# Moving one group's attention stage one to three beats later in a decoder-layer kernel, with the exponential's table loaded ahead of the first softmax

## The reference, cut to what matters

```
# stage 1, linear attention: 16 heads of 8
q, k = sigmoid(n @ Wq + bq), sigmoid(n @ Wk + bk);  v, h = n @ Wv + bv, n @ Wh + bh
attn = (q (k^T v)) / (q sum(k));  gated = layernorm(attn) * (h + beta)
x1   = x + relu(gated @ Wo + bo)
# cross attention to ctx (128 keys of width 96), 16 heads of 64
x2   = x1 + softmax(Q K^T / 8) V @ XWo + Xbo,   Q from layernorm(x1), K and V from ctx
# feed-forward: a shared one and the best of 8 experts
out  = x2 + shared(layernorm(x2)) + expert[argmax](layernorm(x2))
```

## Time and profile before

| | us |
|---|---|
| median of three runs | 604.29 (603.48 to 604.79) |
| the profiled execution | 604.9 |
| its span | 603.2 |
| PE busy, share of the span | 576.2, 96% |
| DVE busy | 432.7, 72% |
| ACT busy | 432.1, 72% |
| POOL busy | 306.9, 51% |
| share of PE in the chain that ended last | 67% |
| mean granted TensorE clock | 0.993 of full |

### The profile page before, as it was taken

The page is one execution under the profiler, slowest core; times in us unless marked ns, Lnnn a source line. Parts: engine busy times, 40 slices in busy tenths (PEclk is TensorE's granted clock), DMA queues, the critical chain, the costliest instruction groups (busy, mean ns, idle before and its releaser), DMA issues.

```text
span 603.2 us, 15181 instructions
## 1 busy us (share of the span) xinstructions
PE 576.2 (96%) x5479; PEld 529.2 (88%) x5479; DVE 432.7 (72%) x1214; ACT 432.1 (72%) x1514; POOL 306.9 (51%) x328
## 2 busy tenths in 40 slices
PE   7978999999999999999999999999999999999993
PEld 7867998998999899988899898988998988899893
DVE  3868666878686768766877777676857459689773
ACT  2668778777876777676867687768776876777771
POOL 3544653365336743475256544563365336246774
PEclk9998999999999999999999999999999999999998
DMA  7530000000000000010000000000040021252530
GB/s 153 136 76 14 18 2 1 15 19 2 1 15 28 28 2 14 19 33 6 14 20 26 11 2 15 19 19 2 24 136 20 7 65 37 68 144 80 151 101 15
DMA packets 24955, 23.52 MB, mean 39 GB/s; under 512 B 7007, under 2 KB 22497, under 8 KB 24880
## 3 DMA queue, kind: packets, MB, share of 16 engines
q1 hardware_dynamic: 21520, 15.96, 10.1%
q0 software_dynamic: 2784, 6.32, 3.0%
q10 hardware_dynamic: 576, 0.26, 0.6%
HBM read 15.03 MB, written 7.95 MB: 38 GB/s over the span
## 4 chain that ended last, share of the span: by engine, by line
PE 67%; ACT 16%; DVE 10%; DMA 3%; issue 2%; POOL 1%; SPq 1%; POOLq 0%; DVEq 0%
PE bank L1451 8%; PE bank L1429 8%; PE bank L1416 8%; PE bank L1440 8%; PE bank L1277 7%; ACT prob L1147 7%; PE bank L1279 6%; PE bank L1278 6%; PE bank L1565 4%; PE bank L1295 2%; PE bank L1397 2%; PE bank L1582 2%; ACT probT L1153 2%; PE bank L1283 2%; ACT L1118 1%
## 5 line engine op out<-in xcount | busy, mean ns | idle before, releaser
L1147 ACT ACTIVATE prob<-bank,mneg 128x128 f32<-128x128 f32 x512 | 183.3, 387 | 65.1 <-DVE mneg L866 64.9
L604 POOL TENSOR_TENSOR prob<-prob,rden 128x512 f32<-128x512 f32 x124 | 126.6, 1041 | 102.7 <-DVE rden L873 102.6
L1147 ACT ACTIVATION_READ_ACCUMULATOR prob<-bank,mneg 128x1 f32 x512 | 115.3, 225 | 0.0
L1153 ACT COPY probT<-bank 128x512 f32<-128x512 f32 x128 | 77.6, 608 | 16.3 <-PE bank L1429 15.6
L866 DVE TENSOR_REDUCE mneg<-bank 128x4 f32<-128x512 f32 x128 | 83.0, 670 | 2.7 <-PE bank L1416 2.5
L1429 PE MATMUL bank<-ident,prob 128*128 128x128 f32 x512 | 78.4, 276 | 1.8 <-ACT probT L1153 0.7
L543 POOL TENSOR_TENSOR rstd<-var_eps,neg_half 128x4 f32<-128x4 f32 x24 | 24.7, 1030 | 99.1 <-DVE var_eps L700 99.1
L1429 PEld LDWEIGHTS bank<-ident,prob 128*128 128x128 f32 x512 | 59.8, 142 | 8.4 <-issue 2.9
L1416 PE MATMUL bank<-kT,qT 64*128 64x128 f32 x1024 | 65.9, 279 | 0.0
L1416 PEld LDWEIGHTS bank<-kT,qT 64*128 64x128 f32 x1024 | 59.8, 188 | 5.8 <-issue 2.5
L1451 PE MATMUL bank<-xwo,oT 128*128 128x128 f32 x512 | 63.7, 277 | 0.4 <-issue 0.4
(11 more groups left out here) (225 smaller groups left out, 1391.3 us busy)
## 6 DMA issues: line engine op xcount, KB each, us to landing
prob<-routed SPq DMA_DIRECT2D x39, 128.5 KB, 2.3
s_work<-in_x_dram SPq DMA_DIRECT2D x8, 256.0 KB, 2.9
ctx_nat<-in_ctx_dram SPq DMA_DIRECT2D x8, 192.0 KB, 2.6
routed<-blank SPq DMA_DIRECT2D x9, 128.5 KB, 3.5
s_work<-in_L_ffn_rt_gate_dram SPq DMA_DIRECT2D x1, 1024.0 KB, 5.5
s_work<-in_L_ffn_rt_up_dram SPq DMA_DIRECT2D x1, 1024.0 KB, 9.5
prob<-in_L_xattn_Wq_dram SPq DMA_DIRECT2D x1, 512.0 KB, 6.8
xwo<-in_L_xattn_Wo_dram SPq DMA_DIRECT2D x1, 512.0 KB, 9.7
```

Of the source, the lines that this page charges most:

```text
L604: nc.gpsimd.tensor_tensor(view, view, spread(rden[:, m % 2, c * NC:(c + 1) * NC], 2, S), ALU.mult)\
L1147: last = nc.scalar.activation(prob[:, m % 2, p * S:(p + 1) * S], score_bank[c][:, i * S:(i + 1) * S], ACT.Exp, bias=mneg[:, m % 2, p:p + 1 ...
L1153: nc.scalar.copy(probT[:, m % 2, c * 512:(c + 1) * 512], made(r1, ("T", m, c))[:])\
```

## The change

It adds entries for group 1 to `MOVED`, changes one, moves the two halves of the feed-forward's weight split, and adds one activation that makes the compiler load the exponential's table there.

```
@@ MOVED
-                 (1, "turn x"): (-2, 3), (1, "copy x^T"): (-2, 3), (1, "x^T low"): (-2, 3),
+                 (1, "turn x"): (-2, 3), (1, "copy x^T"): (-2, 3), (1, "x^T low"): (-1, 0),
...
+                 (1, "sigmoids"): (-1, 3), (1, "k^T v"): (0, 0), (1, "mask"): (0, 0), (1, "q k^T v"): (0, 1),
+                 (1, "attention"): (0, 1), (1, "gate terms"): (0, 0), (1, "rstd of attention"): (0, 1),
+                 (1, "gating, first half"): (0, 2), (1, "gating, second half"): (0, 2),
+                 (1, "turn gated"): (1, 0), (1, "copy gated^T"): (1, 0), (1, "output"): (1, 1), (1, "x1"): (1, 1),
+                 (1, "rstd of x1"): (1, 1), (1, "normalise x1"): (1, 1), (1, "turn x1"): (1, 3),
+                 (1, "x1^T high"): (1, 3), (1, "x1^T low"): (1, 3)})
@@ DVE, loop over (n, b)
-                    if (n, b) == (-1, 3):
+                    if (n, b) == (1, 2):
                         dve.wait_ge(wm_hi, 1)
                         nc.vector.tensor_tensor(sh_gu_lo[:], rawgu, sh_gu_hi[:].bitcast(F32), ALU.subtract)\
@@ ACT, step "x1^T high"
                     nc.scalar.copy(xn2T_hi[:, g % 2], made(r1, (g, 12))[:]).then_inc(hi_in[1], 1)
+                    if g == 0:
+
+                        nc.scalar.activation(table_first[:], neg_half[:], ACT.Exp)
@@ ACT, loop over (n, b)
-                    if (n, b) == (-1, 2):
+                    if (n, b) == (-2, 2):
                         act.wait_ge(wm_in, 16 * 4)
                         nc.scalar.copy(sh_gu_hi[:], rawgu).then_inc(wm_hi, 1)
```

More of the change, by code:

```diff
@@ L347, in decoder_layer @@
                  (1, "stats of x"): None, (1, "rstd of x"): (-4, 2), (1, "normalise x"): (-4, 3),
-                 (1, "turn x"): (-2, 3), (1, "copy x^T"): (-2, 3), (1, "x^T low"): (-2, 3),
+                 (1, "turn x"): (-2, 3), (1, "copy x^T"): (-2, 3), (1, "x^T low"): (-1, 0),
                  (1, "project first pair"): (-1, 0), (1, "first pair"): (-1, 0),
-                 (1, "project second pair"): (-1, 1), (1, "second pair"): (-1, 1)})
+                 (1, "project second pair"): (-1, 1), (1, "second pair"): (-1, 1),
+                 (1, "sigmoids"): (-1, 3), (1, "k^T v"): (0, 0), (1, "mask"): (0, 0), (1, "q k^T v"): (0, 1),
[4 more added lines that the diff above has]
+                 (1, "x1^T high"): (1, 3), (1, "x1^T low"): (1, 3)})
         def steps_at(table_, starts, n, b):
```

## The result

The changed kernel takes 608.49 us (median of four runs, 607.93 to 608.89), against 604.18 us for the kernel before on the same chip (603.48 to 604.79): 1.0075 times the time, interval 1.0063 to 1.0087, or 4.3 us more. That is the forecast's side, and 0.6 us above the upper end of its range. The profiled execution took 608.7 us with a span of 607.0, 3.8 more than before's 603.2.

A forecast was written before the change was run, and what follows sets the result against it. PE, 96% busy, bounds the kernel, so only the first 63 us can win or lose time. Sequence 3's scores 1.6 us late, less 0.2 for gating, gave 604.29 + 1.4 = 605.7 us; range 601.8 to 607.9.

The forecast's parts named there:

- What bounds the kernel: PE, busy 96% of the span; from 63 us on, earlier gains or losses arrive at the end one for one.
- The early table, about 0: Exponential table's 1.28 us load moves into ACT's 2.09 us idle stretch; bounds gain 0.4, loss 0.3, taken as 0.
- The weight split, at nothing: Low part, 1.3 us of DVE, moves to slot 1 beside POOL passes DVE waits for anyway; costed at nothing.
- Scores of sequence 1: Start 2.4 earlier, 47.8 against 50.16 us, after a PE wait of about 2.0 us and a clock fall.
- PE's wait for the context's low part: In slot 0, the second value half waits for context low until 57.9, leaving PE idle 1.2 us.
- Attention and the list on VectorE: Attention starts 5.3 later, at 54.1 us; then 10.1 us of DVE work without pause, ending at 64.2.
- x1: Slot 1: 6.5 later and on the path; PE waits 1.4 and again around turn x1; sequence 3's scores 1.6 late.
- Gating: On DVE, 0.2 us less, because POOL's passes will not fall on its halves as unluckily as before.
- the sum: 1.6 late at sequence 3's scores less 0.2 for gating: +1.4, 605.7 us; bounds +0.3 and +2.6.
- Rival (a): At turn x1 in slot 1: x1's variance by 70.0 us, lead kept; -1.7, 602.6 us; chance 0.30.
- rival (c): Clock falls a second time, at the waits around turn x1; adds about 1.7, 607.4 us; chance 0.13.
- Rival (b): Clock stays up, nothing else changes; sequence 3's scores start at 75.7; no change, 604.3 us; chance 0.17.

The follow-up runs named there:

- e4: Changed kernel without the small parts (early exponential table, x^T low a beat later, weight split moved): only group 1's steps from sigmoids to x1^T low moved; ratio 1.0044.
- e7: Kernel before with only the small parts (early table, x^T low, weight split), the split's low part in (2, 1) instead of (1, 2); ratio 0.9997.
- e14: Changed kernel with dummy matmuls in both PE waits, as e9, and the weight split's low part moved to (2, 1); ratio 1.0014.
- e9: Changed kernel with 7 dummy matmuls in PE's wait ahead of the first turn and 5 ahead of turn x1; ratio 1.0016.
- e2: Changed kernel with 12 dummy matmuls ahead of turn x1 in slot 1; ratio 1.0041.
- e11: Changed kernel run again, unchanged, on another chip; 621.34 us against 617.68 for the kernel before, ratio 1.0060.
- e13: Changed kernel with 7 dummy matmuls in PE's first wait and none ahead of turn x1; ratio 1.0035.
- e5: Kernel before with 8 dummy matmuls in PE's wait for the sigmoids, ahead of k^T v; ratio 0.9984.
- e3: Kernel before with only the small parts (early table, x^T low a beat later, weight split's low part in (1, 2)), group 1's stage not moved; ratio 1.0013.
- e12: The same kernel as e7, run again unchanged; 616.13 us against 617.68 for the kernel before, ratio 0.9980.
- e6: Changed kernel with 6 dummy matmuls ahead of turn x1 in slot 1; ratio 1.0035.
- e10: As e8, but VectorE's four normalise operations stand ahead of the reciprocal that lets POOL begin on sequence 2's probabilities; ratio 1.0028.
- e8: Changed kernel with group 1's normalise x1 taken from POOL and given to VectorE; ratio 1.0074.

## Why the prediction was right about the side and wrong about the size

**What bounds the kernel** held: all that changed arose by 81 us and arrived at the end one for one (3.4 us late there, 3.8 at the last instruction).

**The early table, about 0**, held in the changed kernel: it lies in ACT's idle stretch and takes 1.28 us again:

```profile
33.97 1.28 ACT L1138 ACT_TABLE_LOAD   x1
...
39.74 0.37 ACT L1157 ACTIVATE prob<-bank,mneg 128x128 f32<-128x128 f32 x1 [1.18 <-DVE mneg L873]
...
46.22 1.28 ACT L1125 ACT_TABLE_LOAD   x1
47.51 0.63 ACT L1125 ACTIVATE s_work<-s_work 128x512 f32<-128x512 f32 x1
```

The first exponential starts 0.25 us sooner, counted from the scores of sequence 0 (1.91 us behind them, 2.16 before). At the scores of sequence 1 the small parts cost 0.4 us (e4 8.36, changed kernel 8.80), the loss side of the forecast's bounds, but at the scores of sequence 2 the two are equal. What I missed is that these parts have a value in the other order: with the sigmoids where they were, they take 0.6 us off the wait and the clock doesn't fall (e7).

**The weight split, at nothing**, was wrong by 0.33 us. I named POOL's passes as its cover. They are what VectorE waits for, but the split doesn't lie beside them for free: it lengthens the pass that turn x1 waits for. At the fourth mile post that is worth 0.2 to 0.3 us (e14 against e9, e4 against the changed kernel).

**Scores of sequence 1** were forecast at 47.8 and came at 46.63. The wait was right (T at 45.45, found 45.36), but the clock didn't fall behind it in this execution. Where it fell as forecast, as the first turn began, the post is the forecast one: 9.75 in e2, with 9.7 forecast. In e11 it fell only as the scores began; they started as early as here and took 3.66 us. Either way the scores of sequence 2 were 2.2 to 2.3 us ahead by the mile posts (e2, e11), with 2.3 forecast. PE's wait for the context's low part, forecast at 1.2 us, was 1.4 there and 0.16 in the changed kernel, where VectorE had come early.

**Attention and the list on VectorE**: 54.1 forecast, 52.26 found, early by the clock again; 10.1 us of list forecast, 10.3 found (52.26 to 62.57). **x1**: variance 10.7 us behind the scores of sequence 2 forecast, 10.95 found; waits of 1.4 and 0.5 forecast around turn x1, 1.42 and 0.43 found. The lead was lost where I had said, to the releaser I had named.

**Gating**, at 0.2 less "because POOL's passes will not fall on gating as unluckily as they did before", was wrong: its halves took 2.05 and 1.14 us, here and in e11, against 2.06 and 1.13; the first one again lay beside POOL's probabilities. The term is 0, and the sum +1.6. (Its upper bound should also have read +2.7, 1.4 and the split's 1.3.)

**Rival (a)** (chain in time) had its point of decision at a variance by 70.0 us. It came at 70.23, 1.3 earlier than forecast, and PE waited just as long: what brought the chain forward, the clock, had brought PE forward as well. A point of decision has to be put relative to the engine that waits.

**The step that failed is the clock**: "I expect the clock to fall as it did", at the first wait and there alone, with a second fall as rival (c) at 0.13 and 1.7 us. Rival (b) had the clock up throughout and no change; e9, with the clock up, is 1.1 late. The waits were right; what they do to the clock was taken over from before. By the fourth mile post, against before:

| | us |
|---|---|
| clock up (e9) | +1.1 |
| falls ahead of turn x1, for 3.4 us (e13) | +1.8 |
| falls at the first wait alone (e11) | +2.4 |
| falls behind turn x1 for 6.8 us (changed kernel) | +3.6 |

The forecast described the third row and had +1.6 for it before the gating term, 0.8 short: 0.25 in x1's chain on VectorE, 0.33 in POOL's pass beside the weight split, and 0.2 to 0.3 in the turn and the query piece behind the waits. This last is a thing the rows show once one looks for it: a wait costs more than its idle time, because the matmuls overlap. In the kernel before, where there is no wait, T starts 0.44 us behind turn x1, 0.16 ahead of its end:

```profile
72.05 0.60 PE L1295 MATMUL bank<-ident,xn 128*128 128x128 f32 x4
72.49 0.60 PE L1429 MATMUL bank<-ident,prob 128*128 128x128 f32 x4
```

In e9, with 0.44 of waiting recorded, it starts 1.09 behind, so the wait has cost 0.65. The profiled execution landed on the fourth row. So the forecast of +1.4 missed the measured +4.3 by 2.9: 1.2 for the place and length of the slow stretch, 0.8 for the three terms just named, 0.2 for gating, and 0.7 that the fourth post doesn't show. Rival (c) had the place, but not the size: 2.55 us, where I had counted on 1.7, and it had both falls in one execution, which no run showed. Of the 4.3 us between the medians, 3.4 are there at 81 us and 3.8 at the last instruction of the profiled executions; the last half microsecond is within the spread of the runs, 1.0 us for the changed kernel.

The Trainium skill, page "TensorE: Matmul & The Clock Gate", section "HAM oscillation", says that idle stretches between bursts bring PE back to half clock. The trace agrees that waits of about 2 us can do it, and that filling them stops it (e5, e9); behind the waits of 1.4 us in e3, e7 and e12 the clock stayed up.

**What stays open** is which wait does it. Seven profiled executions have the moved stage and no dummies in the first wait. In four (e2, e6, e10, e11) the clock fell there and not again; in three (changed kernel, e4, e8) it didn't, and fell around turn x1. With the first wait filled it fell at turn x1 (e13). e11 and the changed kernel are the same program with the same waits to 0.01 us. So the forecast of one execution is a mixture of the rows above, and no single row of before could have told which.

## What to carry to other kernels

A wait of 2 us, or two of 1.4 and 0.4 close together, on an engine that is otherwise 96% busy has two prices: its own length, and the slow stretch that it may bring, which cost 0.8 to 2.6 us here and came in one place or another from one execution to the next. When a change trades one such wait for two others, price each of them with and without the slow stretch, and put the worst pair inside the range. And where the chain that decides is two engines long, look at what the change lays beside the slower one: an instruction of 0.7 us on VectorE took a third of a microsecond from POOL's pass.

## What the runs showed of the hardware that I had not expected

VectorE and POOL slow one another down. The weight split (128x512, two operands from SBUF) took between 0.68 and 1.65 us in different places (e7 and e3), and in the changed kernel lengthened a POOL pass from 1.04 to 1.37; four subtractions and products of 128x128 took 1.11 us with POOL idle and 3.48 with POOL busy. The Trainium skill, page "SBUF — State Buffer", section "SBUF: two separate sides", has the two engines share a pair of ports, which whichever starts first holds for a whole instruction, where VectorE's works in a mode with two ports, or has two inputs in SBUF while POOL's reads SBUF. The trace of e8 agrees: each of the first three of the four ends 0.08 us behind the end of one of POOL's three instructions (72.13 and 72.05, 73.13 and 73.05, 74.35 and 74.27 us), and the fourth, beside nothing on POOL, takes 0.34. No run shows in which mode VectorE worked.

The slow stretch of TensorE's clock has no fixed length: 3.4 us in the kernel before, in e11 and in e13, 6.8 us in the changed kernel, and 10.2 us in the last stage of e3.
